# Two-layer attention on one core: all sixteen probability groups of layer 1 split in two parts, two of them copied by SP into doubled sums, and the queries' low part made by VectorE

## The reference

```python
# layer 0 (IC = 64 inner channels)
theta_x = einsum('ic,bcn->bni', theta_w, xf) + theta_b
phi_x   = einsum('ic,bcn->bin', phi_w, xf) + phi_b[None, :, None]
g_x     = einsum('ic,bcn->bni', g_w, xf) + g_b
y       = softmax(theta_x @ phi_x) @ g_x
x       = einsum('ci,bin->bcn', W_w, y^T) + W_b[None, :, None] + xf
# layer 1 (128 channels)
q = einsum('oc,bcn->bno', Wq, xf) + bq
k = einsum('oc,bcn->bcn', Wk, xf) + bk[None, :, None]
v = einsum('oc,bcn->bno', Wv, xf) + bv
x = x + (softmax(q @ k / sqrt(128)) @ v)^T
```

## Time and profile before

| | |
|---|---|
| median of three runs | 3289.11 us |
| the profiled execution | 3288.48 us |
| its span, first to last instruction | 3286.7 us |
| TensorE's granted clock, mean | 0.998 of full speed |
| busy share: PE / DVE / ACT / POOL | 98% / 64% / 58% / 92% |

### The profile page before, as it was taken

The page is one execution under the profiler, slowest core; times in us unless marked ns, Lnnn a source line. Parts: engine busy times, 40 slices in busy tenths (PEclk is TensorE's granted clock), DMA queues, the critical chain, the costliest instruction groups (busy, mean ns, idle before and its releaser), DMA issues. The chain is left out here.

```text
span 3286.7 us, 38831 instructions
## 1 busy us (share of the span) xinstructions
PE 3223.0 (98%) x13636; PEld 2196.9 (67%) x13636; DVE 2094.1 (64%) x3036; ACT 1897.8 (58%) x2473; POOL 3022.9 (92%) x1611
## 2 busy tenths in 40 slices
PE   8999999999999999999999999999999999999997
PEld 5555555557777775555777776555577777777775
DVE  5555555556777765555777776555577777777773
ACT  4554455456666664555566665554566666666665
POOL 6888888898999999888999999998899999999998
PEclk9999999999999999999999999999999999999999
DMA  1000000004665650000466664000057575666666
GB/s 51 26 20 26 23 26 26 23 23 97 126 139 113 141 109 26 26 26 26 95 140 125 134 136 97 20 26 26 26 121 142 116 147 115 127 122 139 121 134 120
DMA packets 91922, 271.45 MB, mean 83 GB/s; under 512 B 10192, under 2 KB 10192, under 8 KB 91728
## 3 DMA queue, kind: packets, MB, share of 16 engines
q0 software_dynamic: 55296, 201.35, 31.9%
q1 hardware_dynamic: 36432, 67.62, 6.7%
HBM read 50.83 MB, written 16.78 MB: 21 GB/s over the span
## 5 line engine op out<-in xcount | busy, mean ns | idle before, releaser
L922 DVE TENSOR_REDUCE piece_max<-rough 128x1 f32<-128x512 f32 x2032 | 1315.8, 684 | 642.9 <-PE rough L510 636.5
L1041 POOL TENSOR_TENSOR p_lo<-probs,p_hi 128x1024 fp32r<-128x1024 f32 x448 | 1235.9, 2822 | 66.5 <-ACT probs L833 59.9
L385 POOL TENSOR_TENSOR sums<-sums,probs 128x1024 f32<-128x1024 f32 x448 | 1066.5, 2381 | 139.6 <-ACT probs L839 101.7
L939 DVE TENSOR_TENSOR probs<-scores,shift_rows 128x1024 f32<-128x1024 f32 x512 | 626.5, 1224 | 488.9 <-PE scores L543 482.5
L839 ACT ACTIVATE probs<-scores 128x1024 f32<-128x1024 f32 x512 | 520.5, 1024 | 681.8 <-PE scores L537 681.3
L832 ACT ACTIVATE p_hi<-probs 128x1024 fp32r<-128x1024 f32 x448 | 474.5, 1059 | 563.3 <-DVE probs L939 563.2
L510 PE MATMUL rough<-keys_a,qry_a 128*128 128x512 f32 x2032 | 705.6, 415 | 32.2 <-DVE piece_max L922 19.6
L510 PEld LDWEIGHTS rough<-keys_a,qry_a 128*128 128x128 f32 x2032 | 368.1, 188 | 347.8 <-DVE piece_max L922 220.4
L833 ACT ACTIVATE probs<-probs 128x1024 f32<-128x1024 f32 x512 | 535.7, 1046 | 88.4 <-DVE probs L939 88.4
L1084 POOL DMA_DIRECT2D sent_sums<-probs x384 | 485.2, 1264 | 0.6 <-issue 0.6
L539 PE MATMUL scores<-qry_a,keys_a 128*128 128x512 f32 x1024 | 447.1, 437 | 0.0
(11 more groups left out here) (94 smaller groups left out, 3175.9 us busy)
## 6 DMA issues: line engine op xcount, KB each, us to landing
sent_sums<-probs POOLq DMA_DIRECT2D x384, 512.0 KB, 5.1
x_q<-x SPq DMA_DIRECT2D x32, 256.0 KB, 2.7
x_res<-x SPq DMA_DIRECT2D x32, 256.0 KB, 3.0
mid<-mid_new SPq DMA_DIRECT2D x32, 256.0 KB, 2.3
x_kv<-mid SPq DMA_DIRECT2D x32, 256.0 KB, 2.8
x_q<-mid SPq DMA_DIRECT2D x32, 256.0 KB, 2.8
x_res<-mid SPq DMA_DIRECT2D x32, 256.0 KB, 3.9
out<-result SPq DMA_DIRECT2D x32, 256.0 KB, 2.8
```

Source lines behind the costliest of these rows:

```text
L385: eng.tensor_tensor(sums[:], sums[:], probs[:, slot(st, s)], ALU.add).then_inc(s_plus, 1)
L922: nc.vector.reduce_max(piece_max[:, t, c:c + 1], src, AX.X).then_inc(s_reduced, 1)
L939: nc.vector.tensor_tensor(probs[:, slot(st, s)].rearrange("p (h c) -> p h c", c=QB), scores[:, s % 2].rearrange("p (h c) -> p h c", c=QB), ...
L1041: nc.gpsimd.tensor_tensor(dst, w, rd(hi), ALU.subtract).then_inc(done, 1)
```

## The change

**All groups split.** `WHOLE`, `HALVED`, `value_group` and the special chunk 1 go. Groups 2 and 3 get a high part on ACT, a low part on POOL, and three F32R products per tile. v_hi and v_lo hold all eight chunks; chunk 1 is split by DVE (or by POOL, for the held values) like the others.

**Sums of layer 1.** `seed` goes. SP copies the probabilities of groups 0 and 1 into the two halves of `sent_sums` with plain DMAs (`copy_probs`), and POOL sends groups 2 to 15. `sent_sums` is doubled, one set for even and one for odd blocks, so a block's copies need not wait for the fold of the block before. Layer 0's `sums` is now the first piece of it. The fold of a layer-1 block after a layer-1 block stands at POOL's step 3.

**Queries' low part.** `q_whole` and POOL's `split_q` go. DVE makes it at the end of a block, from PSUM, with one instruction; PE's second rough piece of the next block waits for it. ACT's remaining copy stands ahead of the last exponential.

**Room.** `diag` shares its place with `rdiag`.

```diff
-FOLD_AT = {None: (None, None), 0: (1, 1), 1: (3, 2)}
+FOLD_AT = {None: (None, None), 0: (1, 1), 1: (3, 3)}
...
-SEEDS = 2
-SEED_AT = {2: 0, 3: 2}
-SENT = tuple(range(4, 16))
+COPIED = (0, 1)
...
-        sums = sb("sums", [P, GC])
-        sent_sums = sb("sent_sums", [P, TPG, GC])
+        sent_sums = sb("sent_sums", [P, 2, TPG, GC])
+        sums = sent_sums[:, 0, 0]
...
         def sent(nth, s):
-            return 16 * (nth * len(SENT) // TPG + (s - SENT[0]) // TPG + 1)
-
-        def v_lows(b, c):
-
-            return b * (BLOCKS - 1) + v_chunk(c) + 1
-
-        def v_chunk(c):
-
-            return c - (c > WHOLE_CHUNK)
+            return 16 * (nth // 2 * (GROUPS - TPG) // TPG + s // TPG)
+
+        def sent_sem(nth, s):
+
+            return s_sent[nth % 2][s % TPG]
+
+        def summed(eng, nth, s):
+
+            if s in COPIED:
+                eng.wait_ge(s_copied[s], 16 * nth + 16)
+            else:
+                eng.wait_ge(sent_sem(nth, s), sent(nth, s))
...
+                eng.wait_ge(sent_sem(nth, 0), sent(nth, GROUPS - 2))
+                eng.wait_ge(sent_sem(nth, 1), sent(nth, GROUPS - 1))
+                both = sent_sums[:, parity]
+                eng.tensor_tensor(both[:, 0], both[:, 0], both[:, 1], ALU.add).then_inc(s_join, 1)
                 eng.wait_ge(s_join, nth + 1)
-                halves = sent_sums[:, 0, 0:QB], sent_sums[:, 0, QB:GC]
+                halves = both[:, 0, 0:QB], both[:, 0, QB:GC]
...
+            def copy_probs(st, s):
+                sp.wait_ge(s_whole, whole_of(st.g, s))
+                if s == COPIED[0]:
+                    sp.wait_ge(s_fold, st.g - (st.prev == 1))
+                settle(sp)
+                sp.dma_start(sent_sums[:, st.parity, s], probs[:, slot(st, s)]).then_inc(s_copied[s], 16)
...
+                if st.layer == 1:
+                    for s in COPIED:
+                        copy_probs(st, s)
...
-            def value_group(st, s):
-
-                pe.wait_ge(s_whole, whole_of(st.g, s))
-                for h in range(TPG):
-                    p = probs[:, slot(st, s), h * QB:(h + 1) * QB]
-                    last = mm(acc_out[:, st.parity], cols(v_vals, s % TPG * TPG + h, KT), p,
-                              start=False, stop=False)
-                last.then_inc(s_used, 1)
...
+                            pe.wait_ge(l_q, st.g + 2)
+                    if m == 1:
+                        pe.wait_ge(l_q, st.g + 2)
...
+                ahead = len(HI_SLOTS)
+                act.wait_ge(s_used, used(st.g, s - ahead) if s >= ahead else used(st.g - 1, s + GROUPS - ahead))
+                if st.prev == 0 and HI_SLOTS[s % ahead] < SHARED_BUFS and s < ahead:
+                    act.wait_ge(s_plus, added(st.prev_nth, GROUPS - SHARED_BUFS + HI_SLOTS[s % ahead]))
+                    act.wait_ge(s_used, used(st.g - 1, GROUPS - SHARED_BUFS + HI_SLOTS[s % ahead]))
+                nc.scalar.activation(hi_part(s), place, ACT.Exp, scale=SCALES[1])
...
-                    if s == GROUPS - 1 and st.next_q:
-                        take_q_whole(st.g + 2, st.next_q[0], two_banks(1))
                     if s == ROW_AT and st.nxt is not None:
                         shift_to_row(st.nxt, st.g + 1, 1 - st.parity)
                     if s == TAKE_AT and st.prev is not None:
                         layer, g, _, parity = before(st)
                         take_output(g, parity)
+                    if s == GROUPS - 1 and st.next_q:
+                        act.wait_ge(s_scores, (st.g + 1) * GROUPS)
+                        take_q_hi(st.g + 2, st.next_q[0], st.parity, two_banks(1))
                     if st.layer == 0:
                         probs_direct(st, s)
-                    if s == GROUPS - 1 and st.next_q:
-                        act.wait_ge(s_scores, (st.g + 1) * GROUPS)
-                        take_q_hi(st.next_q[0], st.parity, two_banks(1))
...
+            def split_q(g, layer, parity, src):
+
+                dve.wait_ge(h_q, g + 1)
+                nc.vector.scalar_tensor_tensor(out=qry_b[:, parity], in0=src, scalar=(TH_B, Q_B)[layer],
+                                               in1=rd(qry_a[:, parity]), op0=ALU.add,
+                                               op1=ALU.subtract).then_inc(l_q, 1)
...
+                if st.next_q:
+                    split_q(st.g + 2, st.next_q[0], st.parity, two_banks(1))
...
-            def seed(st, s):
-
-                pool.wait_ge(s_whole, whole_of(st.g, s + 1))
-                if st.prev == 1:
-                    pool.wait_ge(s_fold, st.g)
-                nc.gpsimd.tensor_tensor(sent_sums[:, s // 2], probs[:, slot(st, s)], probs[:, slot(st, s + 1)],
-                                        ALU.add).then_inc(s_seed, 1)
-
             def send(st, s):
                 pool.wait_ge(s_whole, whole_of(st.g, s))
-                if s - TPG not in SENT:
-                    pool.wait_ge(s_seed, seeded(st.nth, 2 * (s - SENT[0])))
-                else:
-                    pool.wait_ge(s_sent[s % TPG], sent(st.nth, s - TPG))
+                summed(pool, st.nth, s - TPG)
                 settle(pool)
-                nc.gpsimd.dma_start(sent_sums[:, s % TPG], probs[:, slot(st, s)],
-                                    accum_op=ALU.add).then_inc(s_sent[s % TPG], 16)
+                nc.gpsimd.dma_start(sent_sums[:, st.parity, s % TPG], probs[:, slot(st, s)],
+                                    accum_op=ALU.add).then_inc(sent_sem(st.nth, s), 16)
...
-                    if st.layer == 1 and s in HALVED:
+                    if st.layer == 1:
                         split_probs(st, s)
-                    if st.layer == 1 and s in SENT:
+                    if st.layer == 1 and s not in COPIED:
                         send(st, s)
-                    if st.layer == 1 and s in SEED_AT:
-                        seed(st, SEED_AT[s])
-                    if s == Q_LO_AT and st.nxt is not None:
-                        split_q(st.g + 1, 1 - st.parity)
...
-                        if c != WHOLE_CHUNK:
-                            split_held(stage.made * BLOCKS + c, c)
+                        split_held(stage.made * BLOCKS + c, c)
```

116 lines of the change are left out of this document (37 added, 79 removed).

## The result

The changed kernel took 3297.72 us, the median of eight runs (3296.84 to 3298.9), beside 3288.82 for the kernel before (3287.32 to 3289.45): ratio 1.0028, 95% interval 1.0017 to 1.0039. It is slower, by 8.9 us: 0.28%, a small difference but clear of the spread, since no run of the one kernel reaches a run of the other. Its profiled execution has a span of 3295.9 us, 9.2 above the 3286.7 of before.

A forecast was written before the change was run, and what follows sets the result against it. PE was taken to set the pace, POOL close behind. Terms 8 - 1.8 - 1.4 + 3.2 + 0.9 + 1.7 gave +10.6 us: 3299.1 from the profiled execution, 3299.7 from the median; range 3284 to 3311.

The forecast's parts named there:

- The wait: At a regular layer-1 block's denominators, PE waits 0.9 us for POOL's `total`, now behind group 2's split, send and join.
- The send: POOL's send of group 2, ahead of the fold, holds POOL's list for 0.85 us.
- The free send: Rival: the send runs beside POOL's next subtraction, PE does not wait and keeps 0.55 us a block; 3274 us, chance 0.13.
- POOL keeps up: POOL's work in a plain layer-1 block is 54.5 of 55.6 us; late after the fold, it catches up by the last groups.
- The rival of late copies: SP's copy 0 lands after 3115.46, delaying send, fold and PE in 26 blocks; at 0.5 us late 3313 us, chance 0.12.
- 26 regular blocks: Layer-1 blocks behind layer-1 blocks, without three exceptions: 0.9 us wait less 0.6 saved, +0.3 each, +8 us in all.
- last blocks of stages 2 and 4, beyond regular: Without the queries POOL brings the last keys' low part about 0.5 us sooner, PE comes 0.3 later: -1.4 us for both.
- first block of stage 7: POOL's backlog plus group 2's split and send make the fold 5.2 us later; 2.0 comes back by the block's end: +3.2.
- second block of stage 7: It starts with what is left of the first block's backlog: +0.9 us, the regular 0.3 in it.
- last block: POOL's chain ends the program: two more splits and sends (6.56 us) for two seeds (4.8), +1.7 us.
- PE's saving: Splitting groups 2 and 3 shortens PE's weight loads by 0.24 and 0.35 us, 0.6 us in a layer-1 block.
- the rival that it evens out: Wait is only 0.6 us, or some of DVE's 1.7 us rough-piece waits vanish; regular blocks 0, total 3292 us, chance 0.2.

The follow-up runs named there:

- experiment 1: Changed kernel with the layer-1 fold one step earlier, at POOL's step 2, ahead of group 2's split and send: 3287.77 us, ratio 0.9992 to the kernel before.
- experiment 2: Changed kernel with only group 2's send moved behind the fold, its split still ahead: 3281.86 us, ratio 0.9977 to the kernel before.
- experiment 8: Experiment 1's kernel with group 3 of every layer-1 block kept whole, so POOL makes one split fewer: 3277.52 us, ratio 0.9968 to the kernel before.
- experiment 12: Experiment 8's kernel with held values' chunks 5 to 7 moved three steps later in stage 7's first block: 3279.52 us, ratio 0.9973 to the kernel before.
- experiment 11: Changed kernel with held values' chunks 5 to 7 moved three steps later in the first block of stage 7: 3296.37 us, single run.
- experiment 4: Kernel before with only the queries' low part moved to DVE, without POOL's subtraction and ACT's second copy: 3284.10 us, ratio 0.9984.
- experiment 10: Changed kernel with layer 1's residual load cut from 512 to 64 columns: 3298.17 us, single run.

## Why the prediction came out as it did

The forecast was +10.6 us on the profiled execution; measured, +9.2. Its central steps, the wait and the cost of the send, are shown right; that the total came so near is in part luck, as the table below shows.

- **The wait.** POOL's chain came out within 0.07 us at each of its four points, the loads of the denominators at 18.41 where 18.35 stood. Experiments 1 and 2 take the cause away, and the wait shrinks or goes.
- **The send.** 0.85 us was taken from the ends of records, and 0.9 is what moving it gave back. The free send is out. The Trainium skill ("DMA: Bandwidth & Descriptors", Anatomy of one DMA) calls descriptor generation small; in this case what a send holds of POOL's list is measured, and the measurement decides.
- **POOL keeps up, but only just.** In the changed kernel it does. It has about a microsecond, and experiments 1, 8 and 12 show what that margin is worth. The prediction held POOL's work against the block's length, and left late landings out of that sum.
- **Openings of stages 2, 4, 6:** -0.66, -0.68, -0.67 where -0.6 each was said.
- **DVE's low part, ACT's high parts, SP's copies:** nothing, as said. The rival of late copies is dead at 3.6 us to landing.

The terms that were mis-sized:

| term | predicted | measured |
|---|---|---|
| 26 regular blocks | +8 | +2.8 (24 of them: +2.6) |
| openings | -1.8 | -2.0 |
| last blocks of stages 2 and 4, beyond regular | -1.4 | +0.2 |
| first block of stage 7 | +3.2 | +5.5 |
| second block of stage 7 | +0.9 | +0.1 |
| last block | +1.7 | +1.3 |
| layer 0 | 0 | +1.4 |
| sum | +10.6 | +9.2 |

(The parts are rounded.) So the total is nearer than its parts: errors of -5.2 us in the regular blocks and of +2.3 in the first block of stage 7, with +1.6 and +1.4 in the last blocks of stages 2 and 4 and in layer 0, have opposite signs.

**A regular block: +0.1, not +0.3.** The wait is 0.95 where 0.9 was said. The term that was mis-sized is PE's saving, 0.6. From the denominators' first load to the second score load behind group 3 before takes 3125.64 - 3119.26 = 6.38 us, after 3133.59 - 3128.01 = 5.58: 0.80 saved, and the blocks give 0.84. Without a wait it is 0.67: in experiment 1 the same distance is 5.71. Its sixth block of stage 7, from 3100.91:

```profile
3118.37 1.09 PEld L586 LDWEIGHTS acc_out<-ones,total 128*128 128x128 f32 x8
3119.38 0.19 PEld L551 LDWEIGHTS acc_out<-p_hi,v_hi 128*128 128x128 f32 x1
...
3120.65 0.19 PEld L531 LDWEIGHTS scores<-qry_a,keys_a 128*128 128x128 f32 x1
```

Group 2's six loads take 1.27 us there, not the 1.36 of other split groups that the prediction used: some 0.08 more saved, wait or no wait. The other 0.12 is lent by the wait: behind it the first value load follows the denominators' first by 0.89 us (3128.90 - 3128.01), without it by 1.01, before the change and in experiment 1 alike. Why PE's loads do so no run shows. The sentence "no engine lends the time back" was true of the engines and not of PE itself. Two tenths a block, times 26, are the five microseconds by which this term is off. In size the regular block lies nearer to the 0 of the rival that it evens out than to the forecast's +0.3. The rival's mechanism is not what happened: it wanted a wait of 0.6, or DVE's waits to vanish, and these stand as before:

```profile
PEld rough L502 <- DVE piece_max L892: 1.7, 4, 0.5
```

**The first block of stage 7: +5.5, not +3.2.** The backlog was right: loads at 25.21 us, 25.1 worked out. From there to the block's end 37.2 were said and 39.45 came. The sixth block of the same kernel, with the same instructions, shows where the time went. There the distance from the denominators' first load to the second score load behind group 3 is 5.58 us. Here that score load is this one:

```profile
2856.73 0.19 PEld L532 LDWEIGHTS scores<-qry_a,keys_b 128*128 128x128 f32 x1
```

The distance is 2856.73 - 2848.67 = 8.06 us, 2.48 more, and PE waits for no other engine in it. For the first 5.4 us of it the granted clock is low (0.51 until 2854.1), against 1.00 in the sixth block. From that load to the block's end the two take the same, 31.39 and 31.35 us. In experiment 11, where the wait was 3.04 us and the block's mean clock 0.97, the first distance is 7.18, 1.6 more. In experiment 8, at full clock, the way from the denominators to the end takes 58.77 - 20.02 = 38.75 with 1.34 us of waiting in it, so 37.4 with one group whole. So the term that the prediction lacked is the low clock behind the long wait, 2.5 us. No run changed the clock alone, but these are the same instructions in one execution, and the clock is what differs. The prediction read the clock of before, 1.00 in this block too, and took it as given.

**The last block of stage 4** was worked out from POOL's saved subtraction. That step holds (experiment 4: -0.81), and -0.47 and -0.28 in experiments 10 and 11 fit the prediction's -0.4. In the profiled execution a send stood 1.4 us for an earlier send, which took 8.5 us to land where the median is 5.2, and that took it away. Why it landed late in that execution stays open. The 0.67 us of the block behind it is the same lateness. There PE's denominators stood 0.85 us for POOL's `total`, against 0.21 in experiment 10:

```profile
2035.05 0.97 PEld L586 LDWEIGHTS acc_out<-ones,total 128*128 128x128 f32 x8 [0.85 <-issue]
```

**The last block** is at +1.3 for +1.7, but not by the terms of the sum alone. Experiment 4 takes 1.05 us off it by the queries' part, which the sum has at nothing there, so the rest of the change costs some 2.3, an estimate from these two numbers. In the changed kernel PE's denominators stand 3.57 us in this block, where it was 0.75, and a stretch of low clock follows (0.83 over 3236 to 3246). How much of that reaches the end, no run here separates. The same block is at +3.3 in experiment 1 and at +2.5 in experiment 2; why stays open.

**The second block of stage 7** starts with no backlog, for the longer first block gave POOL the time to come level. Experiment 11 fits: with a first block 2.1 us shorter the second is 2.8 longer. **Layer 0** is a miss of 1.4: 0.67 in the block behind stage 4, and 0.77 in the program's first block, whose clock is low for longer in the same first 80 us (before, then after). In the other profiled kernels that start with the same code as the changed one this block is longer by 0.12 (experiment 1) to 1.07 (experiment 10), so most of it belongs to the execution:

```profile
0.00:80.00 80.00, 66.30 (x269) 40.80 (x270) 44.83 (x70) 40.48 (x59) 49.26 (x29) 0.98 0.16 53
```

```profile
0.00:80.00 80.00, 67.02 (x268) 41.39 (x268) 46.44 (x72) 38.80 (x56) 46.27 (x27) 0.96 0.16 53
```

## What to carry to other kernels

Before moving work ahead of a result that another engine waits for, add up the ends along the one list that makes the result: four instructions, read from records of the same kind, gave this wait within a tenth of a microsecond. Two engines at 98% and 92% are a pair: giving back 0.35 us a block of the first for 2.4 us on the second was the best trade here, because slack there swallows late landings. And a wait's price isn't its length: of the regular block's 0.95 us PE took 0.12 back at once, and the 4.30 us of the first block of stage 7 cost 2.5 us more at the low clock. Last, set each term beside its measurement, and not only the sum: here a total that was right to 1.4 us hid a term that was off by five.

## What the runs showed of the hardware

- Around waits of TensorE of 4.30 and 4.22 us stand stretches with a mean granted clock of 0.51 (6.9 us) and 0.57 (7 us); with that of 3.04 goes a smaller shortfall (0.97 over the block, against 0.95). The first of them made the same loads take 8.06 us instead of 5.58. In experiment 1 0.64 and 1.28 us of idle within three microseconds were followed by a low clock too (0.66 over 5 us), and in experiment 8 two of 1.10 and 1.34 weren't. The length of one wait doesn't decide it alone; what does stays open here.
- An accumulating DMA of 512 KB, issued by POOL, holds its list for 0.85 to 0.9 us (rows of before, experiment 2). How long it takes to land (5.2 us in the median) depends on what else moves: in experiment 1 47 of 448 took more than 7 us, without seven eighths of the residual's 256 KB 19 did.
- A DVE addition of two SBUF operands of 128x512 took 2.70 us on average beside POOL's subtractions and 0.69 us without them.
